# TensorE's state sums of a Mamba scan: batches of 16 time steps in every second slot, in place of 8 in each

## The reference

```
def step(h, inputs):
    d_t, B_t, C_t, u_t = inputs
    dA = jnp.exp(d_t[:, :, None] * A)
    h = h * dA + (d_t * u_t)[:, :, None] * B_t[:, None, :]
    y_t = jnp.einsum('bdn,bn->bd', h, C_t)
    return (h, y_t)
```

## Time and profile before

| | |
|---|---|
| median of 3 runs | 2592.97 us |
| the profiled execution, time | 2592.87 us |
| the profiled execution, span | 2591.1 us |
| TensorE / weight loads busy | 2185.0 us (84%) / 1299.1 us |
| VectorE busy | 2148.8 us (83%) |
| ScalarE busy | 1561.4 us (60%) |
| GpSimd busy | 1163.7 us (45%) |
| scans, line 1335 | 512, mean 2340 ns |
| state sums, line 1032 | 8192 records, 565.9 us busy |

### The profile page before, as it was taken

How to read it: one execution, slowest core, us unless ns; L and a number is a source line. 1 busy time by engine, 2 the same in 40 slices (tenths; PEclk the granted TensorE clock), 3 DMA queues, 4 the chain that set the end, 5 groups by cost and what they waited for, 6 DMA issues and landing times. The chain is left out here.

```text
span 2591.1 us, 52242 instructions
## 1 busy us (share of the span) xinstructions
PE 2185.0 (84%) x16672; PEld 1299.1 (50%) x16672; DVE 2148.8 (83%) x2951; ACT 1561.4 (60%) x2746; POOL 1163.7 (45%) x569
## 2 busy tenths in 40 slices
PE   4561999999999898998999983999999989988887
PEld 2230233333333333333333332888888878888776
DVE  7574999999999999999999984777777787777775
ACT  4553988888888888888888861333343333433332
POOL 3314354555545546455454543444444444444332
PEclk7675799999999999999999996999999999989988
DMA  4676211212112121121121213000100020000000
GB/s 113 194 220 192 43 40 37 47 32 45 40 35 48 33 43 41 33 49 35 39 44 30 50 42 110 1 0 0 33 1 0 0 66 1 0 1 5 8 4 17
DMA packets 355498, 114.94 MB, mean 44 GB/s; under 512 B 283000, under 2 KB 346112, under 8 KB 355168
## 3 DMA queue, kind: packets, MB, share of 16 engines
q1 hardware_dynamic: 350672, 110.85, 17.6%
q10 hardware_dynamic: 4752, 3.15, 0.4%
HBM read 68.04 MB, written 45.88 MB: 44 GB/s over the span
## 5 line engine op out<-in xcount | busy, mean ns | idle before, releaser
L1335 DVE TENSOR_TENSOR_SCAN arena<-behind 128x1040 f32<-128x1040 f32 x512 | 1169.5, 2340 | 34.0 <-ACT behind L870 33.8
L924 ACT ACTIVATE arena<-PS,arena 128x512 f32<-128x512 f32 x512 | 348.6, 689 | 621.2 <-PE PS L1110 620.2
L860 ACT ACTIVATE behind<-PS 128x512 f32<-128x512 f32 x1024 | 557.2, 596 | 183.9 <-DVE arena L1335 154.4
L870 ACT ACTIVATE behind<-PS 128x512 f32<-128x512 f32 x1024 | 586.0, 638 | 4.8 <-PE PS L1016 2.3
L1032 PE MATMUL PS<-arena 128*32 128x128 f32 x8192 | 565.9, 407 | 17.5 <-DVE arena L1335 17.5
L1122 PEld LDWEIGHTS PS<-arena 128*128 128x128 f32 x4096 | 472.8, 192 | 7.7
L1122 PE MATMUL PS<-arena 128*128 128x128 f32 x4096 | 473.1, 275 | 0.0
L1110 PE MATMUL PS<-parts_xh,parts_w 128*128 128x512 f32 x1536 | 410.2, 423 | 13.9 <-DVE parts_w L1355 11.4
L1016 PE MATMUL PS<-arena 96*128 96x512 bf16 x1024 | 384.7, 396 | 36.9 <-ACT behind L870 3.5
L1005 PE MATMUL PS<-arena,Ast 96*128 96x512 bf16 x1024 | 332.9, 395 | 60.4 <-DMA arena<-dl_d 33.3
L1032 PEld LDWEIGHTS PS<-arena 128*32 128x32 f32 x8192 | 236.9, 120 | 225.9 <-issue 135.9
(11 more groups left out here) (111 smaller groups left out, 1487.9 us busy)
## 6 DMA issues: line engine op xcount, KB each, us to landing
dl_d<-arena SPq DMA_DIRECT2D x48, 256.0 KB, 3.3
du_d<-arena SPq DMA_DIRECT2D x48, 256.0 KB, 3.5
arena<-dl_d SPq DMA_DIRECT2D x512, 24.0 KB
arena<-b_d SPq DMA_DIRECT2D x64, 192.0 KB
arena<-du_d SPq DMA_DIRECT2D x512, 24.0 KB
b_d<-arena SPq DMA_DIRECT2D x48, 128.0 KB, 2.1
u_d<-arena SPq DMA_DIRECT2D x8, 512.0 KB, 5.2
sz_d<-arena SPq DMA_DIRECT2D x8, 512.0 KB, 5.8
```

The source lines that it names most:

```text
L860: nc.scalar.activation(seg(dA[:, half])[:, j * GI:(j + 1) * GI, 1:], PS[:, j, :].rearrange("p (i t) -> p i t", t=TC), ACT.Exp).then_inc(ex ...
L870: nc.scalar.activation(seg(dB[:, G_])[:, :, 1 + OCT * oct_:1 + OCT * (oct_ + 1)], PS[:, 2 + oct_ % 2, :].rearrange("p (t d) -> p d t", d=G ...
L924: nc.scalar.activation(hT[:, e % 2, c], PS[:, HIDDEN[(GT * e + c) % 3], :], ACT.Gelu, bias=bias1[:, lp, e * GT + c:e * GT + c + 1]).then_i ...
L1335: nc.vector.tensor_tensor_scan(hb[kk][:, q * QD * SEG:(q + 1) * QD * SEG], dA[:, q % 2], dB[:, G_, lo:lo + QD * SEG], 0.0, ALU.mult, ALU.a ...
```

## The change

The sums are issued only in odd slots (1, 3, 5, 7), 16 time steps at a time, where they were issued in all eight, 8 steps at a time. The number of sums and all of their operands stay the same. The sums for a block still run within the slots of the following block; those of the very last block still run in one piece behind the loop.

```
+        SUMS = NQ // 2
...
-                for step in range(part * TC // NQ, (part + 1) * TC // NQ):
+                for step in range(part * TC // SUMS, (part + 1) * TC // SUMS):
                     i, j = step // 4, step % 4
...
-                if part == NQ - 1:
+                if part == SUMS - 1:
                     last.then_inc(y_done, 1)
...
-                    if held(chunk) or kk:
-                        sum_states(*((c, pair, 0) if kk else (c, 0, 1) if pair else (c - 1, 1, 1)), q)
+                    if q % 2 and (held(chunk) or kk):
+                        sum_states(*((c, pair, 0) if kk else (c, 0, 1) if pair else (c - 1, 1, 1)), q // 2)
...
-            for part in range(NQ):
+            for part in range(SUMS):
                 sum_states(NC - 1, BP - 1, 1, part)
```

## The result

The changed kernel takes 2639.0 us (median of 4 runs, 2636.49 to 2644.6) against 2593.39 us before (4 runs): the ratio is 1.018, with a 95% interval of 1.0162 to 1.0197. The forecast was 2638 us. The profiled execution is the slowest of the four, 2644.6 us with a span of 2642.8 us. It is 51.7 us longer than that of before; some 46.2 of them lie between the first scan and the post-work of the last chunk, 1.1 ahead of that and 4.4 behind it. Nothing was changed outside, and another execution of the same kernel (e0_after) has the same scan stage within 0.6 us, but a span of only 2637.2 us; so these 5.5 us look like scatter.

A forecast was written before the change was run, and what follows sets the result against it. VectorE was taken as the bound, with little to spare and ScalarE at the same pace. 2592.9 us + 39 at full clock + 6 for the clock gave 2638 us; 8-in-10 range 2608 to 2656 us.

The forecast's parts named there:

- The chain of the arguments: Odd slots: 0.92 us more sums against 0.46 us slack holds ScalarE up 0.46 us; slot pairs 4.89 us, not 4.42.
- The block with kk = 0: Three slow slot pairs delay the next block's first scan from 680.60 to 681.54: 0.94 us lost a block.
- Two of the signs: kk = 0: ScalarE's exponentials wait 0.3 to 0.5 us; VectorE at block boundaries waits near 1 us for line 871.
- ScalarE's own pace: Two exponentials and two copies per slot were taken to need 2.21 us, ScalarE's own limit.
- My working: At the kk = 0 block's end, slot 7's longer batch ends at 681.48, covered by 0.06 us before the 681.54 scan.
- The projection: Block with kk = 1: the projection, behind late arguments, starts at 655.29 instead of 654.99; 0.30 us lost a block.
- The clock: TensorE's clock falls behind the thin stretch, slowing slot 1: 0 to 0.45 us a chunk, 0.2 taken, 6 us in all.
- the start of the stage: The first block with sums, without post-work, was taken to lose about 0.9 us.
- The hidden delay: Rival: the longer batch costs 0.60 us, hold-up 0.14 a pair drowns in ScalarE's waits; 2593 us, no change; chance 0.09.
- the 0.2 us a pair: Rival: fewer changes of matmul tiling save TensorE 0.2 us per slot pair; 2581 us at best; chance 0.04.
- The low clock through the whole stage: Rival: even slots without sums keep TensorE at 1.2 GHz, pairs 5.5 us; some 270 us lost, to 2860; chance 0.05.
- One reason given against it: Around 286 us, the clock was said to rise at once when sums came, with the same matmuls beside them.

The follow-up runs named there:

- e1: Changed kernel's 16 sums per odd slot replaced by 4 in even and 12 in odd slots, all computed; 2597.41 us, 1.0011 against the kernel before.
- e8: Changed kernel's 16 sums per odd slot replaced by 2 in even and 14 in odd slots, all computed; 2637.11 us, 1.0166 against the kernel before.
- e4: Changed kernel with half of the sums left out: 8 per odd slot, none in even slots; 2592.8 us, 0.9993 against the kernel before.
- e5_clock: Changed kernel plus two unread matmuls in slot 0 of kk = 0 blocks, from the second chunk on; 2628.92 us, 1.0142 against the kernel before.
- e3_even: Changed kernel with the 16 sums in each even slot and none in odd ones; 2607.85 us, 1.0049 against the kernel before.

## Why the prediction was right

*The chain of the arguments* was right, shown by the trace (T + 2.76 for T + 2.77, pairs of 4.88 for 4.89) and by e1, e8 and e4: the loss is there when the batch between products and arguments outlasts the chain's 0.46 us of slack, whether the other slots are empty or not, and absent when it does not. The block with kk = 0 lost 0.97 us at full clock, for 0.94. Two of the signs came out otherwise: ScalarE's waits for arguments are 0.75 us and not 0.3 to 0.5, and the wait of near 1 us at the boundary is for the last sums (line 1033) and not for line 871. Both have the same reason:

*ScalarE's own pace* was wrong, without harm. I took 2.21 us for its limit; held up, it does a slot in 1.97. The 2.21 us of the earlier trace rows was the pace of the scans (2.25). Within a pair this cancels, since the loop runs through the copies' end. But the copies of slot 7 then end 0.2 us earlier than in my sum:

```profile
696.01 1.22 ACT L871 ACTIVATE behind<-PS 128x512 f32<-128x512 f32 x2
695.57 2.04 PE L1033 MATMUL PS<-arena 128*32 128x128 f32 x32
```

The copies end at 697.23, the last sums at 697.61, and the scan starts at 697.73: it waits for `y_done`. My working had the sums ready 0.06 us before the scan would start anyway; in fact they are last, and 36.2 us of waits stand under them. The length of the block comes out the same within 0.1 us (21.72 for 681.54 - 659.85 = 21.69), since the working had the sums end at nearly the same time.

*The projection* had the right mechanism and too large a price. It now starts right behind the arguments, 14.90 us after the first scan of its block (712.63 - 697.73), for 14.98 in the working and 14.68 before. But its matmuls then take 0.61 us and not 0.71, which the working did not have, and the post-work behind them comes 0.11 us later (15.54 against 15.43) and not 0.30:

```profile
712.63 0.61 PE L1050 MATMUL PS<-wout_s,arena 128*128 128x128 f32 x4
```

The block lost 0.12 us. That VectorE's wait ahead of line 1308 grew by 0.29 (1.37 against 1.08) does not bear out the 0.30: 0.17 of it is VectorE being early. During the new wait at the boundary GpSimd gets its copy done (0.29 us at 697.06, line 674; 2.33 at 680.84 before), and the first four scans take 8.97 us, where they took 9.14 beside it.

*The clock* cost more than the 0.2 us a chunk that I took: 41.68 us is the mean of 30 chunks (331.83 to 1582.08), 0.30 above the 41.38 without a fall, some 9 us in all for 6, inside the bounds of 0 to 14. e5_clock shows the same sum (9.8 us) by taking the falls away. In these runs the low clock costs time only where TensorE and ScalarE taking turns set the pace: e4_half, with a short batch, loses nothing, and e1_dose12, whose batch just fills the slack, has falls in nearly every chunk too and loses 0.06 us a chunk. Counted in steps of 1 us from 290 to 1555 us, the clock fell in 26 places, where it was 11 before. The Trainium skill ("TensorE: Matmul & The Clock Gate", HAM oscillation) says that idle gaps between bursts of matmuls let the clock fall back; the trace agrees, with the 0.50 behind the thin stretch, and of the term's 0 to 14 us 9 came.

*Sum.* Per chunk 0.97 + 0.12 + 0.30 = 1.39 us, against 0.94 + 0.30 + 0.20 = 1.44. The trace has 46.2 us in the stage, for a forecast of 45: 42.6 in 30 chunks, and 3.6 ahead of the first `skip` (331.83 - 265.18 = 66.65 us against 327.14 - 264.05 = 63.09), where the working had 0.9 for the first block and 0.94 for the next. There both blocks wait 1.34 us for their last sums (the first scans at 303.18 and 322.94). The total agrees better than its parts: the projection was taken 0.18 us a chunk too high, the clock 0.10 too low and the start of the stage some 1.8 us too low. That these cancel is luck.

*The rivals.* The hidden delay is out by e8 (its 2.01 us batch loses all of it), and by the 149.4 us of waits. The Trainium skill ("TensorEngine Tiling (Array Packing)", Key Properties) says that a change of tiling mode drains TensorE; the 0.2 us a pair that the prediction put against it was worked out from rows, and no run here measures the drain by itself. It is beside the point: TensorE's total was not what ScalarE waited for (0.5 us before, in one slot), and the kernel got slower with half of the changes. The low clock through the whole stage did not come; the chunk's mean clock is 0.96. One reason given against it was read wrongly: the clock did not rise at once when the sums came. The first batch still ran at 0.50 (a row of the timeline, then columns as in the earlier trace rows).

```profile
282.48 1.13 PE L1032 MATMUL PS<-arena 128*32 128x128 f32 x16
282.00:284.00 2.00, 2.00 (x20) 0.78 (x20) 2.00 (x1) 2.00 (x4) 1.88 (x1) 0.50 0.44 100
```

## What to carry to other kernels

An engine with idle time can still hold others up through the order of its queue: before batching work, add up the chain from the event that frees a resource to the instruction that its customer waits for, and see how long a batch may stand between. Here 0.46 us was free, 0.92 was added, and only the excess of 0.46 cost. An engine's own pace cannot be read from slots in which it keeps step with another; it shows where it has to catch up. And a lower clock that is free as long as the queues catch up again costs time in every round once a loop through that engine sets the pace.

## What was not expected of the hardware

**Sums on column tiles go by fours.** 16 records (8 steps) take 1.11 us, 24 take 1.57, 28 take 2.01 and 32 take 2.03; 4 records of two steps take 0.63, 8 records of four steps 0.65. Half clock changes next to nothing in it: 1.13 us for 16 records at 0.50 (282.48, above).

**A GpSimd operation waits for a whole scan, or not at all.** The copy at line 673 takes 0.3 us when VectorE stands still and up to 2.4 us, one scan, when a scan has just begun, and none took a time between: before the change 30 copies of the stage took 0.3 us and 96 took 2.0 to 2.4, after it 83 and 43. Its mean fell from 1794 to 999 ns, for the same 64 columns. The Trainium skill ("SBUF — State Buffer", Terms) says that VectorE and GpSimd share a pair of ports, held for the full instruction, and that the loser blocks; these times agree. What seems to follow is odd: where a scan starts 0.17 us later (e3_even), GpSimd's gate is 1.95 us shorter and the block with kk = 1 0.8 us shorter. I did not try such a gap by itself.
